# Order of TensorE's work at the end of a batch of attention: an output product and two transposes trade places

## The chip, the cores and the metric

The kernel runs on one core of a Trainium2 chip. A core has a matrix engine (TensorE, here PE; its weight loads are listed apart as PEld), VectorE (DVE), ScalarE (ACT), GpSimd (POOL), and SyncE (SP), which issues most DMAs. Each engine takes its own instructions in order and waits on semaphores for the others. TensorE writes its results to PSUM, eight banks of 128 x 512 fp32. The metric is the device time of one execution in microseconds.

## The reference

One transformer layer on x of 16 batches x 512 rows x 512 columns, in fp32: cross attention on a context of the same shape, with 16 heads of 32, then a feed-forward part.

```python
def attention(q, k, v):                      # q = layernorm(x), k = v = ctx
    qh, kh = heads(q @ Wq.T), heads(k @ Wk.T)
    vh = heads(v @ Wv.T + bv)
    scores = einsum('bhsd,bhtd->bhst', qh, kh) * scale
    mask = triu(ones((S, S)), k=0); mask[0, 0] = False   # a row sees only columns before it
    probs = softmax(where(mask, -inf, scores))
    return einsum('bhst,bhtd->bhsd', probs, vh) @ Wo.T + bo
x = x + attention(layernorm(x), ctx, ctx)
h = bitlinear(layernorm(x), w_fc) + gate * (layernorm(x) @ v.T @ fast_b.T @ u.T)
x = x + bitlinear(relu(h) ** 2, w_proj)      # bitlinear: weights rounded to -1, 0, 1 times a row's scale
```

## The kernel before, in words

There are two phases. The attention phase handles one batch at a time: a setup, then fifteen steady batches in a hardware loop, then a last batch written apart. The feed-forward phase follows, with its own loop. Values of fp32 are split in a high and a low part (fp32r), and a product is three products of parts.

In attention the order of all work is one hand-written list of steps per batch, `batch_steps` (lines 57 to 95). Every engine walks through the same list and takes out of it what is its own; the order of two steps in the list matters only for engines that have work in both. A semaphore is waited for by its count. The function `jobs` (line 372) also gives the steps of `MM_STEPS` and their parts a running number n and one of two PSUM banks in turn; a job may start when the job two before it has been read (`mm_free`).

Heads are worked in four groups of four. The steps of a group g:

- Q, K: a projected and transposed piece of queries and keys (12 products); STACK: DMAs that lay it out for the scores.
- S(g, 0..9): ten units of scores with mask on TensorE; VectorE takes the maxima of rows. M(g): TensorE transposes the maxima; ScalarE and VectorE split them; SEND(g): two DMAs write them as two more rows beside the stacked queries.
- T(g, 0..9): ten units of transposed scores, one or two products each, in turn into two PSUM banks. ScalarE takes the exponential of each into `probs` (line 845), POOL zeroes the masked part (line 532). T(g, k) waits for the exponential of T(g, k - 2), which frees its bank (line 744), and T(g, 0) for the DMAs of the maxima.
- ONES(g): sums of `probs` for the groups 0 to 2 (8 products). PV(g, r): probabilities times values; for group 3 with the sums.
- NC, NT, NR, NB, NM, NH, NL: on ScalarE and VectorE, the context of the group is copied out, divided by the sums, and split in `attn` high (NH) and low (NL).

The output of a batch is four row blocks j, each in a bank of its own (`out_bank`). OA(j, g) for g of 0 and 1, OC(j) for group 2 and OB(j) for group 3 each add three products (lines 658 to 663). OA(j, 0) waits for group 0's NL, OA(j, 1) for group 1's. The banks of OA(0, .) and OA(1, .) are those of the scores S, and those of OA(2, .) and OA(3, .) are those of T: OA(2, 0) and OA(3, 0) wait for the last exponential of the batch (line 778).

While a batch ends, the next one is begun: C_LOAD (SyncE) loads the next context, CT(k) transposes a quarter of it on TensorE (four transposes of 128 x 128, line 701, the first of them waiting for the load), ScalarE writes the high part (`cT_hi`, line 826) and VectorE the low part (`cT_lo`, line 908) and frees the bank. The last batch has no next one: `batch_steps(False)` leaves these steps out.

What TensorE does around the change, in the steady batches: M(3), PV(2, .), OA(0,0), T(3,0), T(3,1), OA(1,0), T(3,2), T(3,3), ONES(2), T(3,4), T(3,5), OA(1,1), T(3,6), T(3,7), OA(0,1), T(3,8), T(3,9), CT(2), CT(3), OA(3,0), OA(2,0), OA(3,1), PV(3,0), PV(3,1), OA(2,1), CT(0), CT(1), PV(3,3), PV(3,2), OC(0), K(0), and the rest of OC and OB.

Of the kernel before, what the change touches and what calls it, by code (L numbers as in the profile page):

```python
# [45 lines left out]
def setup_steps():  # L46

    def w(n):
        return [("W", n, k) for k in range(4)]

    return ([("LN_STATS", j) for j in range(4)] + [("LN_VAR",), ("LN_RSTD",)] + w(0) + [("LN_NEWTON",)]
            + [("LN_APPLY", j) for j in range(4)] + [("CT", k) for k in range(4)] + [("XT", k) for k in range(4)]
            + [("W_LOAD",)] + w(1) + [("Q", 0), ("K", 0), ("STACK", 0, 0), ("STACK", 0, 1), ("BV",)] + w(2)
            + [("W_SUM", 0), ("W_SUM", 1)] + w(3) + [("BIAS",), ("W_LIMITS",), ("W_TERN",), ("W_STORE",)])


def batch_steps(more):

    steps = [
# [3 lines left out]
        ("STACK", 1, 0), ("M", 0), ("V", 2), ("SEND", 0), ("PART", "Q", 2, 0), ("STACK", 1, 1), ("PART", "Q", 2, 1),  # L63
# [26 lines left out]
    ]  # L90
    if more:
        return [s for s in steps if s[0] not in ("FFN_WEIGHTS", "FFN_VALUES")]
    return [s for s in steps if (not is_next(s, True) or s[0].startswith("LN_") or s[0] == "XT")
            and s[0] not in ("C_LOAD", "W_LOAD", "W_SUM", "W_LIMITS", "W_TERN", "W_STORE")]


def low_parts_later(steps):

    out, held = [], None
    for k, s in enumerate(steps):  # L100
        if s[0] in MM_STEPS + ("STACK", "M"):
            if held is not None:
                out.append(held)
            ahead = [x[0] for x in steps[k + 1:k + 4]]
            if s[0] in ("Q", "K", "V", "XT", "CT") and "S" in ahead and not any(
                    x in MM_STEPS for x in ahead[:ahead.index("S")]):
                held = s
                continue
            held = None
        out.append(s)  # L110
        if s[0] == "S" and held is not None:
            out.append(held)
            held = None
    assert held is None
    return out


def is_next(step, in_batch):

    return in_batch and (step[0] in ("LN_STATS", "LN_VAR", "LN_RSTD", "LN_NEWTON", "LN_APPLY", "XT", "CT")  # L120
                         or step[:2] in (("Q", 0), ("K", 0), ("STACK", 0)) or step[:3] == ("PART", "Q", 0))
# [112 lines left out]
def attention_phase(nc, shared, dram, batches):  # L234
# [9 lines left out]
    assert W_SHARE == P and PR_ROWS * CHUNKS == P  # L244

    SETUP, STEADY, LAST = setup_steps(), batch_steps(True), batch_steps(False)
    MM0, MMB = count_mm(SETUP), count_mm(STEADY)
    assert MMB % 2 == 0
# [3 lines left out]
    with ExitStack() as c:  # L252
# [119 lines left out]
        def jobs(steps, first, parity):  # L372


            ring = mm_bank + s_bank if steps[0] == SETUP[0] else mm_bank
            n = 0
            for s in steps:
                if s[0] in MM_STEPS:
                    yield s, first + n, ring[(parity + n) % len(ring)]
                    n += 1  # L380
                elif s[0] == "PART":
                    yield s, first + n, ring[(parity + n) % len(ring)]
                else:
                    yield s, None, None
# [9 lines left out]
        def batch_of(step, i):  # L394

            return 0 if i is None else i + 1 if is_next(step, True) else i
# [195 lines left out]
        def _(pe):  # L592
# [71 lines left out]
                return last  # L664

            def program(steps, i, first, parity):
                for s, n, out in jobs(steps, first, parity):
                    b = batch_of(s, i)
                    part = None
                    if s[0] == "PART":  # L670
                        part, s = s[3], s[1:3]
# [121 lines left out]
            transposed, begun, v_job = {}, {}, {}  # L793
            pe.sem_inc(ones_done, START)
            in_loop(pe, program)

        @block.scalar
# [64 lines left out]
        def _(dve):  # L862
            def program(steps, i, first, parity):
                chain = Tally(dve_self, 0 if i is None else i * CHAIN + CHAIN0)
                hi = 0 if i is None else i * (MMB - HI_SKIP) + MM0
                highs = 0
                for s, n, out in jobs(low_parts_later(steps), first, parity):
                    b = batch_of(s, i)
                    if s[0] == "W_LIMITS":
# [597 lines left out]
```

## Time and profile before

| | |
|---|---|
| median of 3 runs | 2622.51 us (2621.42 to 2623.83) |
| profiled execution | 2617.52 us, its span 2615.8 us |
| TensorE busy (PE / weight load PEld) | 2533.3 us, 97% / 1901.9 us, 73% |
| VectorE, ScalarE, POOL busy | 1758.0 us, 67%; 1020.7 us, 39%; 789.5 us, 30% |
| mean granted TensorE clock | 0.994 |

A row of the timeline gives start, duration, engine, line, operation, what it writes and reads, the shape of the first of the instructions merged in it, their count, and in brackets how long the engine had idled before and what ended that. TensorE's products overlap in the array: a product's row is longer than the distance to the next one's start. `bank<-stack 98*128` is T, `bank<-wT,cT_hi` and `bank<-wT,cT_lo` on line 662 are OA and OC, `bank<-ident,xc_rows` are CT and the like, `bank<-acc,ones` is ONES.

### The profile page before, as it was taken

What the parts mean: (1) busy time and instruction counts of PE and PEld (TensorE: products, weight loads), DVE (VectorE), ACT (ScalarE), POOL (GpSimd) and SP (SyncE); (2) the same over time, 40 slices, a digit from 0 to 9 for tenths busy, and PEclk for the clock granted to TensorE, in tenths of its full rate; (3) what the DMA queues carried; (4) which work ended last, traced back from release to release, by engine and by line L of the source; (5) the groups of instructions that cost most, each with busy time, mean ns of one, the idle gap of its engine ahead of it and who ended that gap; (6) DMA issues with size and microseconds to landing.
All of it is one profiled execution on the core that took longest, in us unless ns stands there. A gap on an engine that the chain in (4) does not pass through costs nothing. (4 is left out here: it accounts for less than half of the span.)

```text
span 2615.8 us, 45263 instructions
## 1 busy us (share of the span) xinstructions
PE 2533.3 (97%) x14018; PEld 1901.9 (73%) x14018; DVE 1758.0 (67%) x3492; ACT 1020.7 (39%) x1887; POOL 789.5 (30%) x1499
## 2 busy tenths in 40 slices
PE   6999999999999999999999999999999999999998
PEld 5676676677667667667667657888888888888887
DVE  5676776776776676667677665666666666666663
ACT  2433533433433443353353344333333333333333
POOL 1644643654563473474464360000000000000000
PEclk8999999999999999999999999999999999999999
DMA  4444354264354344344435441111111111111111
GB/s 153 111 125 127 95 141 133 77 161 113 87 147 132 93 122 133 111 111 125 130 92 143 131 117 49 48 48 48 48 48 48 48 48 48 48 48 48 48 50 47
DMA packets 147810, 240.78 MB, mean 92 GB/s; under 512 B 26419, under 2 KB 34611, under 8 KB 147780
## 3 DMA queue, kind: packets, MB, share of 16 engines
q1 hardware_dynamic: 143684, 239.35, 32.1%
q10 hardware_dynamic: 4096, 1.06, 0.2%
q8 instruction: 16, 0.26, 0.0%
q14 instruction: 14, 0.11, 0.0%
HBM read 100.85 MB, written 37.77 MB: 53 GB/s over the span
## 5 line engine op out<-in xcount | busy, mean ns | idle before, releaser
L845 ACT ACTIVATE probs<-bank 128x512 f32<-128x512 f32 x640 | 359.0, 597 | 294.2 <-PE bank L633 288.4
L1238 PE MATMUL h_bank<-xT_hi,wT 128*128 128x512 f32 x1024 | 398.4, 389 | 0.5 <-ACT projT L1269 0.5
L1239 PE MATMUL h_bank<-xT_lo,wT 128*128 128x512 f32 x1024 | 398.4, 389 | 0.0
L1253 PE MATMUL y_bank<-projT,wT 128*128 128x512 f32 x1024 | 398.3, 389 | 0.0
L1255 PE MATMUL y_bank<-projT,wT 128*128 128x512 f32 x1024 | 398.3, 389 | 0.0
L1305 ACT ACTIVATE acc<-h_bank,scale_fc 128x512 f32<-128x512 f32 x256 | 176.4, 689 | 487.4 <-PE h_bank L1242 487.4
L532 POOL TENSOR_SCALAR_AFFINE_SELECT probs<-probs 128x256 f32<-128x256 f32 (+1 forms) x640 | 228.9, 369 | 231.9 <-ACT probs L845 225.4
L608 PE MATMUL bank<-stack 96*128 96x512 f32 (+3 forms) x1024 | 264.1, 335 | 17.4 <-DMA stack<-stage 12.9
L633 PE MATMUL bank<-stack 98*128 98x512 f32 (+3 forms) x1024 | 263.5, 341 | 15.5 <-DMA stack<-m_stage 14.8
L934 DVE TENSOR_REDUCE maxima<-bank 128x1 f32<-128x512 f32 x256 | 175.8, 687 | 126.0 <-PE bank L612 122.8
L1381 DVE CAST wT<-acc 128x512 fp32r<-128x512 f32 x256 | 108.3, 423 | 214.4 <-ACT acc L1310 214.4
L574 POOL TENSOR_TENSOR x_res<-x_res,bias_sb 128x512 f32<-128x512 f32 x64 | 80.6, 1291 | 524.6 <-DMA x_res<-in_x_dram 524.6
L633 PEld LDWEIGHTS bank<-stack 98*128 98x128 f32 x1024 | 171.6, 191 | 91.2 <-ACT probs L845 47.4
L608 PEld LDWEIGHTS bank<-stack 96*128 96x128 f32 x1024 | 176.4, 191 | 70.0 <-issue 22.9
L1238 PEld LDWEIGHTS h_bank<-xT_hi,wT 128*128 128x128 f32 x1024 | 192.2, 188 | 40.5 <-issue 0.6
L1253 PEld LDWEIGHTS y_bank<-projT,wT 128*128 128x128 f32 x1024 | 192.2, 188 | 39.9
L1239 PEld LDWEIGHTS h_bank<-xT_lo,wT 128*128 128x128 f32 x1024 | 192.2, 188 | 39.9
L1255 PEld LDWEIGHTS y_bank<-projT,wT 128*128 128x128 f32 x1024 | 192.2, 188 | 39.9
L826 ACT ACTIVATE stage<-bank 128x512 fp32r<-128x512 f32 x128 | 76.5, 598 | 309.6 <-PE bank L599 284.2
L550 POOL TENSOR_TENSOR acc<-probs 128x384 f32<-128x384 f32 x192 | 190.4, 1012 | 12.7 <-POOL probs L532 8.4
L1383 DVE TENSOR_TENSOR wT<-acc,wT 128x512 fp32r<-128x512 f32 x256 | 177.3, 692 | 8.8
L599 PE MATMUL bank<-cT_hi,wT 128*128 128x512 f32 x512 | 179.1, 410 | 1.5 <-DVE stage L908 1.5
(172 smaller groups left out, 4676.2 us busy)
## 6 DMA issues: line engine op xcount, KB each, us to landing
stack<-stage SPq DMA_DIRECT2D x768, 128.0 KB, 2.3
xc_rows<-in_x_dram SPq DMA_DIRECT2D x16, 1024.0 KB, 5.3
x_res<-in_x_dram SPq DMA_DIRECT2D x16, 1024.0 KB, 5.1
x<-x_res SPq DMA_DIRECT2D x64, 256.0 KB, 2.3
xc_rows<-x SPq DMA_DIRECT2D x16, 1024.0 KB, 5.6
x_res<-x SPq DMA_DIRECT2D x16, 1024.0 KB, 7.5
out_dram<-y_sb SPq DMA_DIRECT2D x64, 256.0 KB, 2.0
xc_rows<-in_ctx_dram SPq DMA_DIRECT2D x15, 1024.0 KB, 5.2
```

Source lines behind the costliest of these rows:

```text
L532: return pool.affine_select(out=view, in_=view, compare_op=ALU.is_ge, fill=0.0, base=0 if first_block else -1, pattern=([[0, count]] if co ...
L550: chain.inc(pool.tensor_tensor(acc[:, h, P:S], probs[:, u0, P:S], probs[:, u1, 0:S - P], ALU.add))
L599: last = pe.matmul(out, a(k), b(k), start=m == 0, stop=m == len(pairs) - 1)
L608: pe.matmul(out[:, cols:cols + t1], st[0:96, QS, h, P * r:P * r + P], st[0:96, KS, h, 0:t1], start=start, stop=False, skip_group_check=True)
L633: return pe.matmul(out[:, cols:cols + S - P * r], st[0:98, KS, h, P * r:P * r + P], st[0:98, QS, h, P * r:S], start=True, stop=True)
L845: act.activation(probs[:, s[2], :], t_bank[u % 2][:, :], ACT.Exp, scale=SCALE).then_inc(exp_done, 1)
L1238: pe.matmul(h_bank[b % 2][:, :], fcT[:, k, cols], xT_hi[:, k, :], start=k == 0, stop=False)
L1239: pe.matmul(h_bank[b % 2][:, :], fcT[:, k, cols], xT_lo[:, k, :], start=False, stop=False)
L1253: pe.matmul(y_bank[j][:, :], a_hi[:, b % RING, P * j:P * j + P], projT[:, b, :], start=b == 0, stop=False)
L1255: last = pe.matmul(y_bank[j][:, :], a_lo[:, b % RING, P * j:P * j + P], projT[:, b, :], start=False, stop=b == NB - 1)
L1305: act.activation(relu[:, b % 2, :], h_bank[b % 2][:, :], ACT.Relu, scale=scale_fc[:, b:b + 1]).then_inc(relu_done, 1)
L1383: dve.tensor_tensor(a_lo[:, b % RING, :], act_sq[:, b % 2, :], a_hi[:, b % RING, :].bitcast(F32), ALU.subtract).then_inc(hid_ready, 1)
```

## The change

In the list, OA(1,0) stands ahead of T(3,0) instead of behind NL(1,0); this holds for the steady and the last batch. Of the engines only TensorE has work in OA. A new function moves CT(2) from behind T(3,9) to behind T(3,1), and CT(3) to behind T(3,5); it is applied in TensorE's program alone and to the steady batches alone. ScalarE and VectorE keep CT at the old places of their lists. The order of the numbered jobs among themselves stays: Q(0), CT(2), CT(3), CT(0), CT(1), so numbers and banks are the same.

```diff
-        ("PV", 2, 2), ("OA", 0, 0), ("NM", 1, 0), ("NH", 1, 0), ("T", 3, 0), ("T", 3, 1), ("NL", 1, 0), ("OA", 1, 0),
+        ("PV", 2, 2), ("OA", 0, 0), ("NM", 1, 0), ("NH", 1, 0), ("OA", 1, 0), ("T", 3, 0), ("T", 3, 1), ("NL", 1, 0),
...
+def context_turned_early(steps):
+
+    out = []
+    for s in steps:
+        if s not in (("CT", 2), ("CT", 3)):
+            out.append(s)
+        if s == ("T", 3, 1):
+            out.append(("CT", 2))
+        if s == ("T", 3, 5):
+            out.append(("CT", 3))
+    return out
...
             def program(steps, i, first, parity):
-                for s, n, out in jobs(steps, first, parity):
+                for s, n, out in jobs(context_turned_early(steps) if steps is STEADY else steps, first, parity):
                     b = batch_of(s, i)
```

TensorE's order after, in the steady batches: OA(0,0), OA(1,0), T(3,0), T(3,1), CT(2), T(3,2), T(3,3), ONES(2), T(3,4), T(3,5), CT(3), OA(1,1), T(3,6), T(3,7), OA(0,1), T(3,8), T(3,9), OA(3,0), OA(2,0), OA(3,1), PV(3,0), and on as before.

## Rows read from the trace of the kernel before

**Rows 1.** Waits on TensorE, 120 to 1540 us: total, times, longest.
```profile
PEld bank L633 <- ACT probs L845: 44.1, 106, 0.8
```
**Rows 2.** Stretches: length, each engine's busy time (instructions), granted clock, DMA share, GB/s.
```profile
120.00:880.00 760.00, 737.07 (x4636) 513.92 (x4629) 530.30 (x1105) 304.58 (x608) 389.06 (x737) 1.00 0.45 119
...
1543.00:1550.00 7.00, 6.08 (x36) 2.35 (x36) 2.78 (x5) 0.90 (x2) 6.73 (x12) 0.53 0.91 346
1550.00:1574.00 24.00, 20.94 (x142) 13.05 (x142) 9.76 (x22) 7.78 (x18) 4.45 (x11) 1.00 0.23 49
```
**Rows 3.** Timeline of TensorE: M(3) of the first and the fifteenth steady batch.
```profile
117.87 0.33 PE L736 MATMUL bank<-ident,maxima 128*128 128x128 f32 x1 [0.15 <-DVE maxima L941]
...
1448.69 0.33 PE L736 MATMUL bank<-ident,maxima 128*128 128x128 f32 x1 [0.16 <-DVE maxima L941]
```
**Rows 4.** Timeline of TensorE, ninth steady batch, 881.3 to 890.2 us.
```profile
881.38 0.40 PE L662 MATMUL bank<-wT,cT_lo 128*128 128x512 f32 x1
882.36 0.74 PE L633 MATMUL bank<-stack 98*128 98x512 f32 x3 [0.58 <-DMA stack<-m_stage]
882.94 0.68 PE L662 MATMUL bank<-wT,cT_hi 128*128 128x512 f32 x2
...
883.68 0.94 PE L633 MATMUL bank<-stack 98*128 98x512 f32 x3
...
885.55 0.74 PE L633 MATMUL bank<-stack 98*128 98x256 f32 x3
886.12 0.63 PE L662 MATMUL bank<-wT,cT_hi 128*128 128x512 f32 x2
...
886.83 0.90 PE L633 MATMUL bank<-stack 98*128 98x384 f32 x3
887.56 0.63 PE L662 MATMUL bank<-wT,cT_hi 128*128 128x512 f32 x2
...
888.26 0.69 PE L633 MATMUL bank<-stack 98*128 98x384 f32 x4
888.78 1.04 PE L701 MATMUL bank<-ident,xc_rows 128*128 128x128 f32 x8
889.93 0.47 PE L662 MATMUL bank<-wT,cT_hi 128*128 128x512 f32 x1
```
**Rows 5.** Timeline of the weight loads in the same batch: T(3,2), T(3,6), T(3,7).
```profile
883.63 0.19 PEld L633 LDWEIGHTS bank<-stack 98*128 98x128 f32 x1 [0.22 <-ACT probs L845]
...
886.74 0.30 PEld L633 LDWEIGHTS bank<-stack 98*128 98x128 f32 x2 [0.19 <-ACT probs L845]
887.23 0.19 PEld L633 LDWEIGHTS bank<-stack 98*128 98x128 f32 x1 [0.19 <-ACT probs L845]
```
**Rows 6.** Timeline of ScalarE: the exponentials of group 3, one of them alone.
```profile
882.98 2.28 ACT L845 ACTIVATE probs<-bank 128x512 f32<-128x512 f32 x4 [1.14 <-PE bank L633]
886.09 2.27 ACT L845 ACTIVATE probs<-bank 128x512 f32<-128x512 f32 x4 [0.83 <-PE bank L633]
...
887.28 0.60 ACT L845 ACTIVATE probs<-bank 128x512 f32<-128x512 f32 x1
...
888.70 1.09 ACT L845 ACTIVATE probs<-bank 128x512 f32<-128x512 f32 x2 [0.33 <-PE bank L633]
```
**Rows 7.** One line's instructions, 120 to 1540 us: duration in ns, min/median/max.
```profile
L701 PE MATMUL bank<-ident,xc_rows x480: 270/272/331, 128.4 to 1532.1; 128*128 128x128 f32 x160
```
**Rows 8.** Timeline of TensorE in the last batch.
```profile
1550.12 0.77 PE L633 MATMUL bank<-stack 98*128 98x512 f32 x3
...
1551.46 0.86 PE L633 MATMUL bank<-stack 98*128 98x512 f32 x3
...
1557.62 0.47 PE L662 MATMUL bank<-wT,cT_hi 128*128 128x512 f32 x1 [0.98 <-ACT probs L845]
```
**Rows 9.** The page's DMA issues: count, KB each, us to landing.
```profile
xc_rows<-in_ctx_dram SPq DMA_DIRECT2D x15, 1024.0 KB, 5.2
```
**Rows 10.** Timeline of the weight loads, ninth steady batch: K(0).
```profile
899.40 0.19 PEld L599 LDWEIGHTS bank<-cT_hi,wT 128*128 128x128 f32 x1 [0.35 <-DVE cT_lo L908]
```
**Rows 11.** Timeline of POOL, ninth steady batch: the last two selections.
```profile
889.46 0.90 POOL L532 TENSOR_SCALAR_AFFINE_SELECT probs<-probs 128x256 f32<-128x256 f32 x2 [0.64 <-ACT probs L845]
```

## The prediction

> **What bounds the kernel now.** I read the page first: TensorE is busy 97% of the span and the next engine, VectorE, 67% (the table of the profile): time is won only where TensorE stops idling or does less, and lost where it waits anew. The change removes and adds no instruction; it orders TensorE's queue anew at one place of each batch of attention. So the question is which wait ends last there. TensorE's waits name the pair to look at: the transposed scores T wait for the exponential that empties their bank, 44.1 us in 106 places of the steady batches, on the weight-load row [rows 1]. The split by stretches gives the steady batches a granted clock of 1.00 [rows 2]. The last group's maxima are transposed at 117.87 us in the first of the fifteen steady batches and at 1448.69 in the last [rows 3], 14 periods of 95.06 us; the batches look alike in the timeline, so one, the ninth, read instruction by instruction, stands for fifteen.
>
> TensorE's order before, with starts [rows 4]: OA(0,0), its third product at 881.38; hole; T(3,0), T(3,1) 882.36; OA(1,0) 882.94; T(3,2), then T(3,3) and ONES 883.68; T(3,4), T(3,5) 885.55; OA(1,1) 886.12; T(3,6), T(3,7) 886.83; OA(0,1) 887.56; T(3,8), T(3,9) 888.26; CT(2), CT(3) 888.78; OA(3,0) 889.93. Three of these starts are set by ScalarE and not by TensorE: a T may start 0.05 us after the exponential two units back has ended. T(3,2) loads its weights at 883.63 and T(3,6) at 886.74 [rows 5]; the exponentials they wait for began at 882.98 and 886.09 and last 0.60 us [rows 6], so they ended at 883.58 and 886.69. OA(3,0) waits for the tenth exponential: the pair T(3,8), T(3,9) begins on ScalarE at 888.70 and is done 1.09 us later, 889.79 [rows 6], and OA(3,0) follows 0.14 us behind.
>
> The reader is to see one more thing: what the two context transposes do at their old place. T(3,9) is issued by 888.78; OA(3,0) couldn't start before 889.93 whatever stood between. The eight transposes take 0.11 us each (eight in 1.04 us [rows 4], of which 0.27 is the last one's own duration [rows 7]: 0.77 / 7) and fill a hole that is there anyway. The last batch has no next context and so no CT: there TensorE idles 0.98 us between T(3,9) and OA(3,0), for the exponential [rows 8]. From T(3,0) to OA(3,0) that batch takes 1557.62 - 1550.12 = 7.50 us, the steady one with both transposes 889.93 - 882.36 = 7.57. Their price at the old place is nothing beyond 0.07 us.
>
> **The change, part by part.**
>
> OA(1,0) moves ahead of T(3,0). It is three products at 0.23 us (882.94 to 883.63), 0.70 us in all. OA(0,0)'s third product starts at 881.38 and is through at 881.61; the maxima's DMA lets T(3,0) go at 882.36, a hole of 0.75 us. OA(1,0) then ends at 882.31 and is hidden, with 0.05 us to spare: no cost to T(3,0). Its operands are those OA(0,0) has already waited for, and its bank is free by then. At its old place 0.70 us go, but T(3,2) behind it waits for the first exponential until 883.63 and started 0.05 us later: the gain is between 0 and 0.05, and I take 0, because the pair T(3,2), T(3,3) must also wait for the second exponential. What is late next is ScalarE.
>
> CT(2) takes its place, 4 x 0.11 = 0.44 us from 882.94 to 883.38, inside the wait until 883.63. Cost 0; if that cover were gone, 0.44. Its input's load is issued ahead of S(3,3) and lands after 5.2 us [rows 9]; seven units of scores and PV(2) lie between. Its bank has long been read.
>
> CT(3) stands behind T(3,5) and ahead of OA(1,1). There nothing waits: T(3,5) is followed by OA(1,1) at 886.12 and T(3,6) comes right behind that, at 886.83, as the exponential frees it (0.05 us after 886.69). So CT(3) pushes OA(1,1) and T(3,6) by 0.44, to 887.27. From there step by step. The exponential of T(3,6) starts 0.45 behind it as before (887.28 - 886.83), at 887.72, and ends 888.32. T(3,7) had waited for its bank until 887.23 [rows 5], and no longer has to: it follows T(3,6) by 0.24, as T(3,9) and T(3,1) follow theirs, so OA(0,1) starts at 887.27 + 0.24 + 0.23 = 887.74 instead of 887.56, and T(3,8) at 888.44 instead of 888.26, free to go since 888.37. Its exponential starts at 888.70 + 0.18 = 888.88. ScalarE keeps 0.49 us between neighbours: that of T(3,7) starts 888.21 and ends 888.81. T(3,9) needs that bank, so it can't start before 888.86, and its exponential 0.54 later (as 885.55 to 886.09), 889.40, or by ScalarE's own pitch 889.37. Before it was 889.19. So the tenth exponential is 0.18 to 0.21 us late; 0.25 of CT(3)'s 0.44 us went into the 0.33 us that ScalarE idled ahead of 888.70 [rows 6]. I take 0.19.
>
> At the old place of CT(2) and CT(3) 1.1 us of TensorE work is gone, but OA(3,0) still waits for the tenth exponential, now until 890.12. Gain 0; the bounds are -1.14 (were OA(3,0) bound by TensorE alone, 889.93 - 888.78) and 0, and the row of the last batch decides for 0.
>
> What lies behind doesn't absorb the 0.19. ScalarE empties CT(2), copies the output bank and empties CT(3) right behind the tenth exponential as before, because its own order is not changed: the transposes are ready early and are not read early. VectorE's row of steps hangs on these copies, and K(0)'s wait at 899.40 for VectorE's low part [rows 10] moves with it. TensorE itself runs from OA(3,0) to PV(3,0) without a hole. POOL has its last selections done at 889.46 + 0.90 = 890.36 [rows 11], while PV(3,0) comes after nine output products of 0.23 us, at 889.93 + 2.1 = 892.0: cover enough. Per steady batch +0.19, in a range of 0 (ScalarE's idle 0.33 takes up more than I think) to +0.44 (it takes up nothing); x 15 = +2.9, from 0 to +6.6.
>
> The last batch gets only OA's move. There TensorE comes to T(3,0) at 1550.12 with no idle ahead of it [rows 8], the stage before having run at a granted clock of 0.53 [rows 2]: the hole that hides OA(1,0) doesn't exist. T(3,0) moves by 0.7; T(3,2), before at 1551.46 behind OA(1,0), now waits for the first exponential: 1550.12 + 0.70 + 0.62 (T(3,0) to its exponential, 882.36 to 882.98) + 0.60 + 0.05 = 1552.09, +0.6 once, between 0 and +1.3 (three products at half clock, twice 0.70, less the 0.05).
>
> **Sum.** +2.9 + 0.6 = +3.5 us on the profiled execution: 2617.5 us (span 2615.8) goes to 2621.0. The median of the runs shown is 2622.5, 5.0 above the profiled one; the same +3.5 gives 2626.0.
>
> A measurement of this kernel tells a difference of about 0.2%, 5.2 us, from no change; +3.5 is under that.
>
> **Rivals.**
>
> *The stage is bound by TensorE's amount of work* (faster). The filled hole is worth its length, and T(3,9) to OA(3,0) shrinks. If only the first hole counts, 15 x 0.58 (the idle shown) = -8.7: 2613.8. For it: 97% busy, and 0.58 us of idle filled for sure. Against it: the last batch's idle of 0.98 us. Chance 9%.
>
> *CT(3)'s delay passes in full* (slower). Place: T(3,6), which was just in time; price 0.44 per batch, 15 x 0.44 + 0.6 = +7.2: 2629.7. It decides from the point at which ScalarE has no idle left between T(3,7) and T(3,8), or T(3,8) starts later than 888.44 because a weight load behind a wait isn't overlapped. Against it: T(3,7)'s own wait and the 0.33 us of idle. Chance 15%.
>
> *Nothing moves*: ScalarE's slack takes it all, and the last batch's cost is hidden. 2622.5 to 2623.1. Chance 9%.
>
> *The clock falls in the new hole* (slower). TensorE will stand still for about 1 us between T(3,9) and OA(3,0) in each steady batch. Where it did fall, ahead of the last batch's tail, 7.00 us ran at 0.53 [rows 2]: 7.00 x 0.47 = 3.3 us lost, at most. If each batch met it, 15 x 3.3 = +50, near 2670; if one or two did, +3 to +7. Against it: the last batch has the same hole of 0.98 us in a stretch of 24 us that holds 1.00, and the steady batches hold 1.00 across idle of up to 0.8 us for an exponential or a DMA [rows 1, 2]. The Trainium skill (TensorE: Matmul & The Clock Gate, "A second HAM failure mode: psum-queue depth-cycling") warns that frequent small idle times of TensorE between groups of products make the clock swing between its two levels; by that rule the sum could go toward 2670, by the rows it stays at 2626. Chance 3%.
>
> The forecast has the remaining 64%.
>
> **Numbers.** 2626.0. Range 2619 to 2630.5: from most of "nothing moves" and the spread of the runs to "in full". Faster by over 0.2%: 9%, all from the first rival. Slower by over 0.2%: half to two thirds of "in full", the clock, and a tenth of the forecast where its two terms are both at their upper side: 21%. Same: 70%.
>
> **What would show it.** In the changed trace, per steady batch: no idle ahead of T(3,0), or under 0.1 us; T(3,2) still 1.27 us behind T(3,0) on TensorE; T(3,6) 0.44 later than now against T(3,0); the tenth exponential 6.40 us behind the first instead of 6.21; a new idle of 0.9 to 1.1 us ahead of OA(3,0), ended by the exponential, 7.7 us behind T(3,0); period 95.25. In the last batch OA(1,0) ends later than 1550.7 and the group runs 0.6 later. I am wrong if OA(3,0) stands less than 7.5 us behind T(3,0), if the granted clock falls inside a steady batch, or if the period doesn't move with the tenth exponential.

## The result, and the profile after

The changed kernel takes 2627.92 us (median of 20 runs, 2619.87 to 2634.11) against 2622.97 (20 runs, 2618.77 to 2626.45) for the kernel before. The ratio is 1.0019, 95% interval 1.0010 to 1.0027: slower by 5.0 us, 2.6 to 7.1. The forecast was +3.5, 2626.0 in a range of 2619 to 2630.5.

The profiled execution of the changed kernel took 2631.33 us, its span 2629.6, 13.8 above the span before, and most of that isn't the change. TensorE in its ninth steady batch (it answers to [rows 4]; T is on line 646 now, OA on 675, CT on 714, ONES on 780):

```profile
887.00 0.33 PE L749 MATMUL bank<-ident,maxima 128*128 128x128 f32 x1 [0.16 <-DVE maxima L954]
...
890.36 0.63 PE L675 MATMUL bank<-wT,cT_hi 128*128 128x512 f32 x2
...
891.09 0.73 PE L646 MATMUL bank<-stack 98*128 98x512 f32 x3
891.66 0.60 PE L714 MATMUL bank<-ident,xc_rows 128*128 128x128 f32 x4
892.35 0.99 PE L646 MATMUL bank<-stack 98*128 98x512 f32 x3
...
894.26 0.73 PE L646 MATMUL bank<-stack 98*128 98x256 f32 x3
894.84 0.60 PE L714 MATMUL bank<-ident,xc_rows 128*128 128x128 f32 x4
895.19 0.70 PE L675 MATMUL bank<-wT,cT_hi 128*128 128x512 f32 x2
...
895.96 0.68 PE L646 MATMUL bank<-stack 98*128 98x384 f32 x3
...
897.18 0.86 PE L646 MATMUL bank<-stack 98*128 98x384 f32 x4
898.85 0.70 PE L675 MATMUL bank<-wT,cT_hi 128*128 128x512 f32 x2 [0.80 <-ACT probs L858]
```

The reader is to see the place of each hole. The one ahead of T(3,0) is gone (no bracket at 891.09), and T(3,0) still stands 4.09 to 4.10 us behind the transpose of the maxima. T(3,2) stands 1.26 behind T(3,0) (its weight load before: 1.27). T(3,6) stands 4.87 behind it instead of 4.47. And 0.80 us of idle has appeared ahead of OA(3,0), ended by the exponential. ScalarE in the same batch, answering to [rows 6]:

```profile
891.70 2.27 ACT L858 ACTIVATE probs<-bank 128x512 f32<-128x512 f32 x4 [1.12 <-PE bank L646]
894.80 1.09 ACT L858 ACTIVATE probs<-bank 128x512 f32<-128x512 f32 x2 [0.83 <-PE bank L646]
896.40 2.31 ACT L858 ACTIVATE probs<-bank 128x512 f32<-128x512 f32 x4 [0.51 <-PE bank L646]
898.59 0.61 ACT L839 ACTIVATE cT_hi<-bank 128x512 fp32r<-128x512 f32 x1
```

Before, the exponentials of T(3,4) to T(3,7) ran as one group of four (886.09 in [rows 6]); now ScalarE idles 0.51 us ahead of T(3,6)'s. The 0.33 us ahead of T(3,8)'s are gone. The last one ends 898.71 - 891.70 = 7.01 us behind the first one's start, against 889.79 - 882.98 = 6.81: 0.20 later. The weight loads answer to [rows 5]: T(3,6) and T(3,7) no longer wait, and T(3,9), which never did, now does.

```profile
892.35 0.19 PEld L646 LDWEIGHTS bank<-stack 98*128 98x128 f32 x1 [0.33 <-ACT probs L858]
...
895.73 0.60 PEld L646 LDWEIGHTS bank<-stack 98*128 98x128 f32 x3
...
897.54 0.30 PEld L646 LDWEIGHTS bank<-stack 98*128 98x128 f32 x2 [0.16 <-ACT probs L858]
```

Where did 13.8 us go? The split by stretches, first of the kernel before, then of the changed one, cut at M(3) of the first steady batch and M(3) of the last batch (columns as in [rows 2]):

```profile
0.00:117.87 117.87, 94.26 (x518) 69.93 (x518) 75.11 (x157) 43.35 (x83) 47.70 (x99) 0.94 0.49 142
117.87:1543.13 1425.26, 1381.38 (x8689) 962.48 (x8689) 995.32 (x2070) 571.21 (x1140) 729.36 (x1378) 1.00 0.45 120
```
```profile
0.00:123.25 123.25, 97.27 (x517) 71.50 (x518) 76.09 (x157) 43.83 (x83) 47.61 (x99) 0.93 0.47 135
123.25:1554.84 1431.59, 1384.27 (x8688) 965.02 (x8688) 994.77 (x2070) 571.16 (x1140) 728.71 (x1378) 1.00 0.45 119
```

5.4 us were lost before the first M(3), where the change has put nothing yet; in the two further profiles of these kernels (below) that M(3) stands at 123.98 for the kernel before and at 118.84 for the changed one. The fifteen batches after it are 6.3 us longer. The remaining 2.1 us lie behind the last M(3): the exponentials of the last batch are 0.55 us late (below), and the mean granted clock of the next 51 us is 0.83 against 0.87. Twelve of the fourteen periods are 95.2 to 95.3; two are not (M(3) of three batches in a row):

```profile
599.58 0.33 PE L749 MATMUL bank<-ident,maxima 128*128 128x128 f32 x1 [0.15 <-DVE maxima L954]
...
694.86 0.33 PE L749 MATMUL bank<-ident,maxima 128*128 128x128 f32 x1 [0.16 <-DVE maxima L954]
...
791.72 0.33 PE L749 MATMUL bank<-ident,maxima 128*128 128x128 f32 x1 [0.16 <-DVE maxima L954]
```

95.28, then 96.86. In the long one the granted clock fell to 0.50 (1.2 of 2.4 GHz) for 3.4 us, and so in the twelfth:

```profile
776.00:780.00 4.00, 2.81 (x21) 1.52 (x19) 2.27 (x4) 2.33 (x5) 2.36 (x5) 1.00 0.88 200
780.10:783.50 3.40, 3.40 (x15) 1.52 (x14) 2.02 (x5) 1.57 (x4) 1.02 (x2) 0.50 0.84 182
...
1258.00:1261.40 3.40, 3.40 (x15) 1.53 (x14) 2.00 (x5) 1.55 (x4) 1.02 (x2) 0.50 0.78 151
```

Ahead of it TensorE had been busy 2.81 of 4.00 us; but it was busy 2.79 to 2.88 us in the same stretch of the other batches too, where no fall followed. Both falls stand 11.6 us ahead of an M(3), in the stretch of PV(1) and the first T and S, and not in the new hole, 11 us behind an M(3). Two such batches cost 1.6 + 1.7 = 3.3 us; 6.3 - 3.3 = 3.0 = 15 x 0.20.

### The profile page after: what moved, and what is told of

It is laid out like the page before. It is cut to its first block and busy times, and to the rows that moved or that the text cites. A ratio compares the mean times of both kernels' runs of the same rounds, so it can differ in the third digit from the quotient of the medians.

```text
span 2629.6 us, 45263 instructions
## 1 busy us (share of the span) xinstructions
PE 2541.0 (97%) x14018; PEld 1907.8 (73%) x14018; DVE 1758.4 (67%) x3492; ACT 1021.2 (39%) x1887; POOL 788.8 (30%) x1499
```

## The experiments

The total time scatters by 10 us and more in either kernel, the periods in a profile by 0.1, so verdicts on a place rest on its rows. The runs list the mean granted clock beside the time. Call (1 - clock) x span the missing clock time: over all 171 runs that list it, one common slope (0.8 us of time for each us of it) and one constant for each kernel leave a scatter of 1.9 us. The third column below is the difference to the kernel before at equal clock by this fit, with its 95% interval. The fourth and the fifth column are medians of the fifteen steady batches (start to start): the tenth exponential and the first product of K(0), each behind M(3). The last is the median of the fourteen periods.

| kernel | ratio to before (95%) | at equal clock, us | tenth exponential behind M(3), us | K(0) behind M(3), us | period, us |
|---|---|---|---|---|---|
| before | | | 10.92 | 21.13 | 95.06 |
| changed | 1.0019 (1.0010 to 1.0027) | +3.6 +- 1.0 | 11.13 | 21.33 | 95.27 |
| ct_behind_t5 | 1.0002 (0.9992 to 1.0012) | +2.1 +- 1.2 | 11.14 | 21.34 | 95.29 |
| oa_and_ct2 | 1.0012 (1.0003 to 1.0022) | +0.3 +- 1.2 | 10.92 | 21.12 | 95.07 |
| oa_only | 1.0005 (0.9992 to 1.0019) | +1.0 +- 1.2 | 10.92 | 21.13 | 95.12 |
| ct3_behind_t7 | 1.0013 (1.0000 to 1.0025) | +5.9 +- 1.2 | 11.35 | 21.56 | 95.49 |
| ct_behind_outputs | 1.0168 (1.0150 to 1.0187) | +44 +- 2 | 10.92 | 24.16 | 98.08 |
| short_chain | 0.9983 (0.9970 to 0.9997) | -3.6 +- 1.2 | 10.69 | 20.89 | 94.82 |
| ones_behind_t5 | 0.9985 (0.9970 to 1.0000) | -2.9 +- 1.3 | 10.71 | 20.92 | 94.87 |
| ones_last | 1.0036 (1.0021 to 1.0051) | +10.3 +- 1.3 | 10.28 | 21.85 | 95.78 |

In every row the period differs from that of the kernel before by what K(0) is early or late, to 0.06 us. K(0) is where VectorE's row of steps comes back to TensorE: it waits for the low part of CT(0) and CT(1). In seven of the nine rows below the first K(0) in turn moves with the tenth exponential; the two others, ct_behind_outputs and ones_last, have a cause of their own in between.

**ct_behind_t5.** OA(1,0) at its old place, and in the function:
```diff
-        if s not in (("CT", 2), ("CT", 3)):
+        if s != ("CT", 2):
             out.append(s)
-        if s == ("T", 3, 1):
-            out.append(("CT", 2))
         if s == ("T", 3, 5):
-            out.append(("CT", 3))
+            out.append(("CT", 2))
```


> One transposed quarter of the context alone is moved, to the place behind T(3,5); the second stays behind T(3,9), and OA(1,0) stays at its old place. My theory (only what stands between T(3,5) and T(3,6) delays the chain of exponentials): the tenth exponential comes 11.12 us behind the transpose of the maxima instead of 10.92, OA(3,0) 11.86 instead of 11.66, the period is 95.25 instead of 95.06, and the last batch is as before (tenth exponential at 13.76). Time +2.9 us. Rival A (the steady batch is bound by TensorE's amount of work, the order doesn't matter): all as before, +0. Rival B (the slowdown comes from OA(1,0) or from both moves together): all as before, +0.

The period and the tenth exponential are those of the full change. Four transposes behind T(3,5) alone make the whole loss of the steady batches. The times themselves don't tell it from nothing; at equal clock it is +2.1, with +2.9 forecast.

**oa_and_ct2.** In the changed kernel:
```diff
-        if s not in (("CT", 2), ("CT", 3)):
+        if s != ("CT", 2):
             out.append(s)
...
-        if s == ("T", 3, 5):
-            out.append(("CT", 3))
```


> The change without its third move: OA(1,0) ahead of T(3,0) and CT(2) behind T(3,1), but CT(3) at its old place behind T(3,9). My theory: all steady batches as before (tenth exponential 10.92 behind the transpose of the maxima, OA(3,0) 11.66, period 95.06), an idle of 0.5 to 0.6 us ahead of OA(3,0), the last batch 0.55 later as in the changed kernel. Time +0.6 us. Rival A (work bound, filled holes pay): period shorter by up to 0.58, up to -8 us. Rival B (the new order of OA(1,0) and CT(2) costs): period above 95.06.

The steady batches are those of before to 0.01 us: the other two moves cost and gain nothing there. The last batch is later, as forecast: its tenth exponential stands 14.27 us behind M(3), against 13.76. Its ratio of 1.0012 is not a cost of the steady batches; its runs had the lowest mean clock of all kernels (0.992), and at equal clock it is +0.3.

**oa_only.** The kernel before with the one row of the list changed.

> Only OA(1,0) is moved ahead of T(3,0). My theory: steady batches as before (period 95.06; a filled hole ahead of T(3,0), and an idle of about 0.7 us ahead of T(3,2) in its place), the last batch 0.55 later (tenth exponential at 14.31 instead of 13.76). Time +0.6 us. Rival A (filled holes pay): 15 x 0.58, -8.7 us.

As expected in the steady batches: a filled hole of 0.58 us, and no gain. The period is 0.06 longer although the tenth exponential and K(0) are on time; that is inside the scatter of single periods, and nothing was run to explain it. The last batch was not 0.55 later (tenth exponential at 13.63 instead of 13.76); more on that below.

**ct3_behind_t7.**
```diff
-        if s == ("T", 3, 5):
+        if s == ("T", 3, 7):
             out.append(("CT", 3))
```


> The changed kernel with CT(3) one pair further back, behind T(3,7) instead of T(3,5). My theory (ScalarE's idle between the exponentials of T(3,7) and T(3,8) has swallowed over half of CT(3)'s 0.44 us, and a transposition behind that pair has nothing left to swallow it): T(3,6) is on time again (exponential 9.01 behind the transpose of the maxima), but the tenth exponential comes at 11.36 (+0.44 against before, +0.24 against the changed kernel), OA(3,0) at 12.10, period 95.5; time +7 us against before, once 0.6 of it in the last batch. Rival (only T(3,6) matters, whichever is late is made up by ScalarE's idle): tenth exponential at 10.92 to 11.12, +0.6 to +3.6 us.

ScalarE in a steady batch:

```profile
893.42 2.27 ACT L858 ACTIVATE probs<-bank 128x512 f32<-128x512 f32 x4 [0.83 <-PE bank L646]
896.46 1.09 ACT L858 ACTIVATE probs<-bank 128x512 f32<-128x512 f32 x2 [0.77 <-PE bank L646]
```

The idle between T(3,7)'s and T(3,8)'s exponential is 0.77 instead of 0.33 us, the full 0.44. The same four transposes cost 0.21 in one place and 0.43 two units later: the difference is what ScalarE's idle had swallowed.

**ct_behind_outputs.** OA(1,0) at its old place, and `if s == ("OA", 3, 1): out += [("CT", 2), ("CT", 3)]` as the only rule of the function.

> CT(2) and CT(3) are moved the other way, from ahead of OA(3,0) to behind OA(3,1), where nothing waits; OA(1,0) at its old place. My theory (at their old place they fill a hole that the tenth exponential makes anyway): OA(3,0) stands at most 0.1 earlier against the transpose of the maxima, with an idle of about 1.0 us ahead of it, and all behind it comes 0.8 to 0.9 us later: period 95.9, +12 to +13 us. Rival A (work bound, order without effect): period 95.06, +0.

The hole is there as expected, and its size:

```profile
914.42 0.69 PE L644 MATMUL bank<-stack 98*128 98x384 f32 x4
916.08 0.71 PE L673 MATMUL bank<-wT,cT_hi 128*128 128x512 f32 x2 [0.98 <-ACT probs L856]
...
918.23 1.03 PE L712 MATMUL bank<-ident,xc_rows 128*128 128x128 f32 x8
```

But the price behind it is 3.0 us per batch and not 0.9. ScalarE has CT(2) ahead of NC(2) in its own order, so it stood still for the late transposes:

```profile
914.85 1.08 ACT L856 ACTIVATE probs<-bank 128x512 f32<-128x512 f32 x2 [0.33 <-PE bank L644]
918.86 0.60 ACT L837 ACTIVATE cT_hi<-bank 128x512 fp32r<-128x512 f32 x1 [2.93 <-PE bank L712]
919.36 0.59 ACT L863 ACTIVATE o_norm<-bank 128x512 f32<-128x512 f32 x1
```

The copy to `o_norm`, for which PV(3,0) waits, starts only at 919.36. But PV(3,0) is only 1.7 us late; the whole 3.0 us stands at VectorE and K(0). VectorE's low part of CT(2) needs ScalarE's high part, and it starts 919.49 - 904.42 = 15.07 us behind M(3) instead of 12.04. All of VectorE's row of steps shifts with it, up to the low part for which K(0) waits. VectorE, then TensorE:

```profile
919.49 0.69 DVE L919 TENSOR_TENSOR cT_lo<-bank,cT_hi 128x512 fp32r<-128x512 f32 x1 [6.64 <-ACT cT_hi L837]
...
928.58 0.50 PE L610 MATMUL bank<-cT_hi,wT 128*128 128x512 f32 x1 [1.27 <-DVE cT_lo L919]
```

I had counted TensorE's own time (+12 to +13 us in all) and not the work queued behind the reader of its result.

**short_chain.** One function gives TensorE's order of this stage as a list, in steady and last batches: OA(1,0), T(3,0), T(3,1), OA(1,1), T(3,2), T(3,3), ONES(2), T(3,4), T(3,5), CT(2), T(3,6), T(3,7), CT(3), T(3,8), T(3,9), OA(0,1), then OA(3,0).

> All of TensorE's side work is laid into the holes that the exponentials leave: OA(1,0), T(3,0), T(3,1), OA(1,1), T(3,2), T(3,3), ONES(2), T(3,4), T(3,5), CT(2), T(3,6), T(3,7), CT(3), T(3,8), T(3,9), OA(0,1), OA(3,0); in the last batch the same without CT. My theory (the chain of exponentials sets OA(3,0)): T(3,8) no longer waits for an output product, so the tenth exponential comes at 10.68 instead of 10.92, OA(3,0) at 11.42 with 0.1 to 0.3 us of idle ahead of it, period 94.8; last batch +0.55 for OA(1,0) and -0.24; time -3.3 us. Rival (work bound): gain by the whole hole, up to -8 us. Rival (CT's place costs, wherever it is): period not below 95.06.

The tenth exponential came at 10.69 and OA(3,0) at 11.42, as forecast. ScalarE runs six exponentials without a pause (M(3) of this batch is at 886.88):

```profile
891.59 2.27 ACT L859 ACTIVATE probs<-bank 128x512 f32<-128x512 f32 x4 [1.12 <-PE bank L647]
894.69 3.46 ACT L859 ACTIVATE probs<-bank 128x512 f32<-128x512 f32 x6 [0.83 <-PE bank L647]
```

This kernel is faster than both, by 0.17% (0.03 to 0.30) against the kernel before. The same transposes that cost 0.21 us ahead of OA(1,1) cost nothing in its place: no T behind them is held up. The 0.55 us expected for OA(1,0) in the last batch did not come: its tenth exponential stands at 13.48.

**ones_behind_t5** and **ones_last** are the same function with other lists: ... T(3,1), CT(2), T(3,2), T(3,3), OA(1,1), T(3,4), T(3,5), ONES(2), T(3,6), T(3,7), CT(3), T(3,8), T(3,9), OA(0,1); and ... T(3,1), OA(1,1), T(3,2), T(3,3), CT(2), T(3,4), T(3,5), CT(3), T(3,6), T(3,7), OA(0,1), T(3,8), T(3,9), ONES(2).

> OA(1,0), T(3,0), T(3,1), CT(2), T(3,2), T(3,3), OA(1,1), T(3,4), T(3,5), ONES(2), T(3,6), T(3,7), CT(3), T(3,8), T(3,9), OA(0,1). The 1.0 us of ONES stands one pair later, with an output product of 0.7 us in its place. My theory: T(3,4) comes up to 0.3 earlier, T(3,6) about as before, the tenth exponential at 10.65 to 10.75, period 94.75 to 94.85, -3 to -4 us. If the DMA of the weights (which waits for ONES) or VectorE's transposed sums come too late, the period is above 95.06.

About as good as short_chain, as expected; the period of 94.87 is just above the 94.75 to 94.85 forecast.

> OA(1,0), T(3,0), T(3,1), OA(1,1), T(3,2), T(3,3), CT(2), T(3,4), T(3,5), CT(3), T(3,6), T(3,7), OA(0,1), T(3,8), T(3,9), ONES(2), OA(3,0): the sums fill the hole ahead of OA(3,0). My theory: T(3,4) and all exponentials behind it come 0.5 to 0.7 earlier, OA(3,0) at 11.0 to 11.2 instead of 11.66. The period gains that (94.4 to 94.6, -7 to -10 us) only if ScalarE's sums of the weights, whose DMA is issued behind ONES, aren't late; if they are, ScalarE's copies behind them hold up VectorE and the period is as before or longer.

OA(3,0) stands at 11.01 and the tenth exponential is 0.64 earlier, but the period is 95.78. Of the two cases the expectation named, it is the bad one: the DMAs of the weights write the tile that ONES reads, so they are issued behind it, now at 895.59 and 896.02, and ScalarE, which sums up the weights, waits for them. The kernel before has no such wait. ScalarE, VectorE, then TensorE, in a steady batch with M(3) at 884.29:

```profile
898.68 0.63 ACT L843 ACTIVATE acc<-acc 128x512 bf16<-128x512 f32 x1 [2.05 <-DMA acc<-in_L_ffn_w_proj_dram]
...
900.57 0.69 DVE L997 TENSOR_TENSOR attn_lo<-o_norm,attn_hi 128x512 fp32r<-128x512 f32 x1 [1.70 <-ACT attn_hi L870]
...
905.94 0.50 PE L613 MATMUL bank<-cT_hi,wT 128*128 128x512 f32 x1 [1.11 <-DVE cT_lo L922]
```

ScalarE's copy to `attn_hi` stands behind that work in its order, VectorE waits 1.70 us for it, and K(0) then waits 1.11 us for VectorE. That the sums of ONES themselves reach VectorE late (it idles 6.77 us for them) isn't what costs: its product behind them, `o_norm`, starts 13.89 us behind M(3), against 14.37 before.

**before_again, after_again.** Both kernels unchanged, profiled once more.

> The kernel before, unchanged, profiled once more. My theory on the scatter (TensorE's granted clock falls to half for a few us at places where it always has little to do, now in one batch and now in another, in either kernel): periods of 95.0 to 95.1 us except in the batches with a fall, which are 1.5 to 1.7 longer; falls in steady batches stand 10 to 12 us ahead of the transpose of the last group's maxima. Rival (falls in steady batches are the change's doing): none in steady batches here.

> The changed kernel, unchanged, profiled once more. My theory: periods of 95.25 us except in batches with a fall, no fall in the new hole ahead of OA(3,0), and a count of falls as in the kernel before, 0 to 3 in the steady batches. Rival (the new hole brings falls): a fall 8 to 12 us behind the transpose of the maxima, or more than three in steady batches.

The kernel before met falls too, two inside steady batches, 11.6 us ahead of an M(3) each; the changed kernel met none between the first M(3) and the last batch, and ran 2620.6 us against 2624.8. The kernel before, then the changed one:

```profile
589.30:592.70 3.40, 3.40 (x14) 1.47 (x14) 2.02 (x5) 1.57 (x4) 1.02 (x2) 0.50 0.74 201
```
```profile
118.84:1547.89 1429.05, 1381.56 (x8688) 963.81 (x8689) 995.91 (x2070) 570.76 (x1140) 728.88 (x1378) 1.00 0.44 120
```

1429.05 without a fall against 1425.26 without a fall before is +3.8. The fourteen periods carry 2.9 of it, 0.21 each. The other 0.9 stands in the one stretch from the last steady M(3) to that of the last batch, 95.35 against 94.43; over all profiles this stretch is up to 0.6 us shorter or longer than the period, and why wasn't looked into. The mean clock over the runs is 0.9930 for the changed kernel (20) and 0.9932 for the kernel before (65). oa_only, whose idle ahead of OA(3,0) is as before, also met two falls in steady batches. In the twelve profiles together 13 falls stand in steady batches, none to two in each, and all of them 11.4 to 11.7 us ahead of an M(3). The falls are a lottery of both kernels.

## Why the prediction was right, point by point

- **Which wait ends last.** Right. OA(3,0) starts 0.14 us behind the end of the tenth exponential in every variant run; TensorE's amount of work had no say (oa_only, oa_and_ct2).
- **OA(1,0) and CT(2): nothing.** Right in the steady batches, shown by oa_and_ct2.
- **CT(3).** Forecast 0.44 for T(3,6) and 0.18 to 0.21 for the tenth exponential; measured 0.40 and 0.21. The forecast that the rest goes into ScalarE's idle is shown by ct3_behind_t7, where nothing is left to take it.
- **Nothing behind absorbs it.** Right: the period grows by what the tenth exponential is late, in each of the three kernels that delay it (0.21 and 0.21, 0.22 and 0.23, 0.43 and 0.43), and shrinks with it in two that bring it forward (0.24 and 0.24, 0.21 and 0.19). The path is the one forecast, over VectorE to K(0).
- **The idle ahead of OA(3,0)** is 0.80 us in the rows, forecast 0.9 to 1.1. T(3,9) itself starts late, for its bank, so less is left; the place of OA(3,0), 7.76 behind T(3,0), is the 7.7 forecast.
- **The last batch, +0.6 once.** Conditional, and the forecast took one execution's state for a property; that it came out in the profiled run is luck. In the changed kernel's first profile T(3,0) stands 1562.51 - 1554.84 = 7.67 behind M(3), against 1550.12 - 1543.13 = 6.99 before, and the exponentials are 0.54 later; in both the clock was low for 6.8 us just ahead of it, and so in oa_and_ct2, which was late too. Where it was low for 3.4 us (the changed kernel again, oa_only) or not at all (the kernel before again, ct3_behind_t7), T(3,0) stands 6.9 to 7.0 us behind M(3), with or without OA(1,0) ahead of it: it comes with the DMA of the maxima, and OA(1,0) hides there too. The changed kernel's first profile, the kernel before again, the changed kernel again:

```profile
1562.51 0.63 PE L646 MATMUL bank<-stack 98*128 98x512 f32 x3
```
```profile
1559.58 0.74 PE L633 MATMUL bank<-stack 98*128 98x512 f32 x3 [2.60 <-DMA stack<-m_stage]
```
```profile
1554.84 0.74 PE L646 MATMUL bank<-stack 98*128 98x512 f32 x3 [0.26 <-DMA stack<-m_stage]
```

- **The sum.** +3.5 forecast, +5.0 measured with 2.6 to 7.1; the rows of the steady batches carry 3.0 and the last batch 0 to 0.55. The other 1.4 to 2 us of the median are not explained; at equal clock the difference is 3.6 +- 1.0, so a different draw of falls in the two sets of runs may be enough. That isn't shown: the twenty runs of the kernel before that the median rests on list no clock, and the fit uses its later runs. That the total came out inside the range is in part luck.
- **The rival "the clock falls in the new hole"** fell: no fall there in any profile. But my test, that I would be wrong if the clock fell in a steady batch at all, was a bad one: such falls belong to both kernels, and one profile without any had made me take 1.00 for a rule.
- **"In full"** is what happens two units later, not here.

## What to carry to other kernels

Work that fills an idle stretch is free only where the stretch has room for it and no link of the chain stands right behind: look for the work that stands ahead of an instruction that starts just as its wait ends. A hole that is filled somewhere is no gain if the engine waits for the same event a little later; ask of each candidate which wait ends last behind it. And when a product is moved later, count what is queued behind its reader on the other engines, and what may start only when its input is free again (the weights' DMAs of ones_last).

## What the runs showed of the hardware that I had not expected

TensorE's granted clock fell from 1.00 to 0.50 for 3.4 us inside stretches that run at 1.00 in all other batches, in none to two of the fifteen batches between the first M(3) and the last of each profile; each such batch was 1.6 to 1.7 us longer. All 13 such falls stand at the same place of the batch, 11.4 to 11.7 us ahead of an M(3). The stretch ahead of it had TensorE busy 2.81 of 4.00 us in a batch with a fall, and 2.79 to 2.88 us in the batches without: what picks the batch isn't known. Runs of the kernel before with a mean clock of 0.990 took 2630.8 to 2633.4 us, those with 0.995 2617.5 to 2621.8: how long the clock is low, in the setup, the steady batches and the last, goes with most of the scatter between executions (3.6 us, of which the fit leaves 1.9).
